# In-degrees counted by VectorE from the edge keys, and one zero piece stored in product 2, in a four-layer graph network

## The reference

```python
agg = jax.ops.segment_sum(h[src], dst, num_segments=n)          # products 0, 1, 2
...
deg = jax.ops.segment_sum(jnp.ones_like(dst, dtype=x.dtype), dst, num_segments=N)
agg = msg_sum / jnp.clip(deg, 1.0, None)[:, None]               # third stage
...
neigh2 = jax.ops.segment_sum(msg2, dst, num_segments=N) / jnp.maximum(deg, 1.0)[:, None]   # last stage
```

## Time and profile before

| | |
|---|---|
| median of three runs | 4858.66 us (4850.25 to 4870.81) |
| profiled execution | 4872.96 us, span of its instructions 4871.1 us |
| PE matmuls busy | 3396.0 us (70%) |
| VectorE busy | 2163.5 us (44%) |
| ScalarE busy | 1955.0 us (40%) |
| GpSimd busy | 1785.8 us (37%) |
| mean granted TensorE clock | 0.842 of 2.4 GHz |

### The profile page before, as it was taken

How to read it: one execution, slowest core, us unless ns; L and a number is a source line. 1 busy time by engine, 2 the same in 40 slices (tenths; PEclk the granted TensorE clock), 3 DMA queues, 4 the chain that set the end, 5 groups by cost and what they waited for, 6 DMA issues and landing times.

```text
span 4871.1 us, 57973 instructions
## 1 busy us (share of the span) xinstructions
PE 3396.0 (70%) x22119; PEld 2919.8 (60%) x22119; DVE 2163.5 (44%) x4433; ACT 1955.0 (40%) x3073; POOL 1785.8 (37%) x1727
## 2 busy tenths in 40 slices
PE   4798888711113997995119999983577777777788
PEld 2676777610113996994019989973465565555666
DVE  8786777510003986884002233242233333333335
ACT  5687878610001444454006546552222222222221
POOL 3000000177772000887760000005665555555630
PEclk9999999855556998996559989996799888888999
DMA  4888888700003677442004424423355555555555
GB/s 152 224 231 238 230 224 232 218 14 4 7 7 77 219 240 251 133 130 37 4 7 150 135 67 149 130 60 108 93 198 187 197 188 182 181 195 196 187 193 180
DMA packets 299723, 712.84 MB, mean 146 GB/s; under 512 B 65270, under 2 KB 167445, under 8 KB 284214
## 3 DMA queue, kind: packets, MB, share of 16 engines
q1 hardware_dynamic: 167180, 436.77, 28.3%
q10 hardware_dynamic: 52298, 174.64, 10.2%
q0 software_dynamic: 79968, 97.68, 9.4%
HBM read 503.59 MB, written 254.50 MB: 156 GB/s over the span
## 4 chain that ended last, share of the span: by engine, by line
PE 47%; another core or an unknown queue 23%; ACT 9%; issue 7%; DVE 7%; DMA 5%; ACTq 1%; DVEq 0%; POOL 0%; SPq 0%; POOLq 0%
PE PS L740 21%; PE PS L1725 7%; DMA turned<-DEG 4%; PE PS L662 4%; PE PS L1711 3%; ACT CA L859 2%; ACT DEG L884 2%; PE PS L1701 2%; PE PS L625 2%; PE PS L1693 2%; PE PS L671 1%; DVE BB L1877 1%; PE PS L718 1%; ACT BB L1811 1%
## 5 line engine op out<-in xcount | busy, mean ns | idle before, releaser
L431 POOL DMA_INDIRECT PAN<-table,src_i x832 | 828.3, 996 | 1353.0 <-DMA table<-DEG 768.1
L972 POOL DMA_INDIRECT shares<-dst_f,spare x832 | 888.2, 1068 | 735.1 <-ACTq L777 427.2
L740 PE MATMUL PS<-CX,XH 125*128 125x376 f32 x2000 | 477.4, 318 | 260.0 <-issue 127.7
L740 PE MATMUL PS<-CX,XL 125*128 125x376 f32 x2000 | 472.7, 315 | 145.1 <-issue 145.1
L1819 ACT ACTIVATE BB<-PS 128x1024 f32<-128x1024 f32 x104 | 106.6, 1025 | 948.5 <-PE PS L1701 473.7
L740 PEld LDWEIGHTS PS<-CX,XH 125*128 125x128 f32 x2000 | 321.1, 197 | 276.8 <-issue 161.2
L740 PEld LDWEIGHTS PS<-CX,XL 125*128 125x128 f32 x2000 | 321.4, 197 | 145.0 <-issue 145.0
L537 ACT ACTIVATE CX<-PAN 125x3125 fp32r<-125x3125 uint8 x106 | 298.2, 2814 | 270.0 <-PE PS L740 233.2
L740 PE MATMUL PS<-CP,XH 125*128 125x376 f32 (+1 forms) x1330 | 313.3, 315 | 124.0 <-issue 79.4
L740 PE MATMUL PS<-CP,XL 125*128 125x376 f32 (+1 forms) x1330 | 309.8, 312 | 63.4 <-issue 63.4
L884 ACT ACTIVATE DEG<-PS 125x1250 uint8<-125x1250 bf16 x250 | 303.0, 1212 | 113.0 <-PE PS L671 61.8
(11 more groups left out here) (334 smaller groups left out, 7026.8 us busy)
## 6 DMA issues: line engine op xcount, KB each, us to landing
PAN<-counts SPq DMA_DIRECT2D x300, 390.6 KB
shares<-SSB ACTq DMA_DIRECT2D x70, 1600.0 KB
XP<-shares SPq DMA_DIRECT2D x50, 1600.0 KB
PAN<-shares SPq DMA_DIRECT2D x50, 1600.0 KB
BB<-start_penalty SPq DMA_DIRECT2D x104, 512.0 KB
shares<-blank ACTq DMA_DIRECT2D x15, 3200.0 KB, 13.9
turned<-DEG SPq DMA_DIRECT2D x50, 781.2 KB, 9.7
PAN<-turned SPq DMA_DIRECT2D x100, 390.6 KB
```

The costliest lines, as they stand in the source:

```text
L431: nc.gpsimd.indirect_dma_start(out=gbuf[g % 2][:, k, :], out_offset=None, in_=source, in_offset=bass.IndirectOffsetOnAxis(ap=src_i[:, t:t ...
L740: last = nc.tensor.matmul(wide_ps[b][h][:, 0:w], halves[part][0:TN, s * SUBJ + j, :], cast_part(v, j, h), start=(s == 0 and j == 0 and par ...
L972: nc.gpsimd.indirect_dma_start(out=shares_flat, out_offset=bass.IndirectOffsetOnAxis(ap=share_at[:, t:t + 1], axis=0), in_=share[:, t:t + ...
```

## The change

VectorE counts the edges of each node from the keys of `dve_window_keys`: for each block and each of the five places in a window, one comparison with a sum (`window_degrees`), 50 in all. The evictions of `take_turn` no longer sum. The degrees lie by windows now (125 partitions, ten blocks, five places), so the store has runs of five elements, and ACT reads the row back by tiles of 125 in `act_in_mean` for use at the end. The build stores six pieces of zeros, three parts in a slice of either width; product 2 stores five slices, one with each of its blocks 0 to 4.

```diff
-ZBUILT = 7
-ZEROS_AT = {"dense1": (1,) * 10, "taken1": 5, "dense2": (0,) * 10}
+ZBUILT = 6
+ZERO_STEPS = tuple(NHI * (i + 1) // (ZBUILT - 2) for i in range(ZBUILT - 3))
+ZEROS_AT = {"dense1": (1,) * 10, "taken1": 5, "dense2": (1,) * 5 + (0,) * 5}
...
-        in_sums = DEG[0:TN, 5728:5728 + TURNS * NBLK * TPB].rearrange("p (c j) -> p c j", c=TURNS)
+        degree_win = DEG[:, 5728:5728 + NBLK * WIN].rearrange("p (q c) -> p q c", c=WIN)
+        degree_junk = DEG[:, 5792:5920]
...
                 if n == 1 and c == 0:
-                    store_degrees(act, 0, rin, rin_ready, rin_out)
+                    act.wait_ge(rin_ready, 1)
+                    act.dma_start(degree_rows[0:1, :].rearrange("o (q p c) -> p (o q) c", p=NWIN, c=WIN),
+                                  rin[0:NWIN, :].rearrange("p (q c) -> p q c", c=WIN)).then_inc(rin_out, 16)
...
                 nc.scalar.activation(to.rearrange("p (b k n) -> p b k n", b=2, n=TN),
-                                     turn_ps[turn_item(k, r) % 2][0:TN, :, :, 0:TN], ACT.Copy,
-                                     accum_out=in_sums[:, m, at:at + 1]).then_inc(turn_taken, 1)
+                                     turn_ps[turn_item(k, r) % 2][0:TN, :, :, 0:TN], ACT.Copy
+                                     ).then_inc(turn_taken, 1)
...
-                    if j in ((12, 24, 36) if k % 2 else (10, 20, 30, 40)):
+                    if j in ((12, 24, 36) if k % 2 else ZERO_STEPS):
                         blank_part()
...
+        def window_degrees(dve, first, count, local, c):
+
+            for x in range(count):
+                placed_after(dve, nc.vector.scalar_tensor_tensor(
+                    out=degree_junk, in0=local[:, x, :], scalar=iota[:, c:c + 1], in1=bc(ones[:, 0:1], 128),
+                    op0=ALU.is_equal, op1=ALU.mult, accum_out=degree_win[:, first + x, c:c + 1]))
...
             elif part == 6:
                 placed_after(dve, nc.vector.tensor_tensor(out=src, in0=src, in1=src_a, op=ALU.add))
+                window_degrees(dve, first, count, local, 0)
...
         def dve_in_degrees(dve):
 
-            dve.wait_ge(turn_taken, TURNS * NBLK * TPB)
-            nc.vector.tensor_reduce(out=rin[0:TN, :], in_=in_sums.rearrange("p c j -> p j c"), axis=AX.X, op=ALU.add)
-            dve.drain()
-            nc.vector.tensor_scalar(rin[0:TN, :], rin[0:TN, :], 1.0, None, ALU.max)
-            dve.drain()
-            nc.vector.reciprocal(rin[0:TN, :], rin[0:TN, :]).then_inc(rin_ready, 1)
+            placed_after(dve, nc.vector.tensor_scalar(rin[0:NWIN, :], degree_win[0:NWIN, :, :].rearrange("p q c -> p (q c)"),
+                                                      1.0, None, ALU.max))
+            nc.vector.reciprocal(rin[0:NWIN, :], rin[0:NWIN, :]).then_inc(rin_ready, 1)
...
         def act_in_mean(act):
 
             spread_degrees(act, 0, A[:, 0:N], rin_out, rin_spread)
+            act.dma_start(rin[0:TN, :], degree_rows[0:1, :].rearrange("o (j p) -> p (o j)", p=TN),
+                          allow_slow_non_contiguous=True).then_inc(rin_out, 16)
...
             keep_nodes(LAST)
+            act.wait_ge(rin_out, 32)
```

More of the change, by code:

```diff
@@ L1121, in dve_window_keys @@
                 placed_after(dve, nc.vector.tensor_copy(hi, whole_i))
+                window_degrees(dve, first, count, local, 1)
             elif part == 9:
@@ L1124, in dve_window_keys @@
                                                                  op0=ALU.mult, op1=ALU.add))
+                window_degrees(dve, first, count, local, 2)
             elif part == 10:
@@ L1127, in dve_window_keys @@
                                                                  op0=ALU.is_ge, op1=ALU.add))
+                window_degrees(dve, first, count, local, 3)
             elif part == 11:
+                window_degrees(dve, first, count, local, 4)
                 nc.vector.scalar_tensor_tensor(out=lo, in0=hi, scalar=-float(TN), in1=src, op0=ALU.mult, op1=ALU.add)
```

## The result

The kernel after takes **4939.85 us** (median of 4 runs, 4938.84 to 4955.68) where the kernel before, on the same chip, takes 4860.49 us (4850.25 to 4870.81). The ratio is 1.0171, 95% interval 1.0141 to 1.0201: slower by about 80 us, clear of the noise though under 2%. Forecast were 4948 us and +89.

The account below looks back on a forecast made before the run. TensorE was taken to bound wide build slices and products, ScalarE the narrow slices, scatter crawl the holes. +116 - 12 - 9 + 6 - 12 = +89 us on 4858.66 gave 4948 us, range 4876 to 4995.

Parts of the forecast that it names:

- The late scatter: Product 2: the scatter's second half starts 155 us later, so 97 columns move behind the product; +116 us.
- The price of 1.292 us a column: Hole after product 2: each column scattered there costs its full time, 272.6 / 211; 97 columns give +125 us of crawl.
- Rival A: After product 2: the crawl ends when product 3 streams, so the late scatter costs 0 to 10 us; 4832 us, 13%.
- The build: Build: ten zero parts removed shorten ScalarE's `turned` wait by 1.2 us a wide slice; -12 us, bounds 0 and -49.
- Rival B: Build: the `turned` waits vanish and all 22 us of ScalarE's reads count; +34 us in all, 4893 us, 12%.
- Accumulator reads: Build evictions: dropping each read saves ScalarE 0.09 us, counted only in the ten narrow slices; -9 us.
- Comparisons: Build: 50 VectorE compares of 0.4 us, +2 before the first pair and +4 in slice 2; +6 us.
- The store of the degrees: Start of product 1: 1250 descriptors instead of 6250 shorten the next DMA issue from 16.78 to 3.4 us; -12 us.
- Stores in product 2 and the reload: Product 2's five added stores lie beside TensorE, product 4's degree reload has only casts after it; 0 each, reload bound +17.

Follow-up runs that it names:

- zeros_in_p1: Against the kernel after: the five zero stores of product 2 are issued in product 1 instead; 4838.17 us, ratio 0.9895 to the kernel before.
- zeros_only: The kernel before with only the new zeros (six pieces in the build, five stores in product 2), old degree counting and store; 4927.43 us, ratio 1.0098.
- degrees_only: The kernel after with the zeros of the kernel before, so only the VectorE degree counting and new store change; 4858.64 us, ratio 0.9965.

## Why the prediction came out as it did

**The late scatter: right, in place and size.** The second half was to start at the end of block 5's casts, 155 us later relative to product 2; it came 153.4 us later (2018.92 - 1930.02 + 64.5). The price of 1.292 us a column, less what TensorE does in it, gave +116; measured 119.7, and `zeros_in_p1` gives about 113 back. Rival A falls: between the steps TensorE crawled on to 2622.90, 23.8 us past the last column.

**The build: right in sign, three times too small.** The step that failed reads "The `turned` store has 2 us more before a third transfer joins. I take 1.2 us a slice". Measured are 5 us a wide slice, of which 3.6 are the wait that I had named (49.4 to 13.1 us in all). I had the right wait and its bound (-49), then sized it by how much later one store is issued, when what mattered was that four stores beside the slice's own transfers were one too many. The two parts run apart put it on the piece of zeros: 45.1 us of this wait with four stores, 11.4 with three. The other sign of it was in the earlier trace rows: TensorE busy 41.05 of 45.20 us at a DMA share of 0.94, so 4 us a slice to be had. (The prediction's "PE and ACT are between 88% and 93% busy" does not hold for ScalarE in the wide slices, 33.40 of 45.20 us or 74%.) With the store gone TensorE's own time fell as well, from 41.05 to 39.56 us, at a granted clock of 0.96 before and 1.00 after: that is the rest of the 5 us. Rival B, which had this, is the better account of the build: it gave -82 with the store, measured -64, though of its 22 us for the reads only 5.6 came.

**Accumulator reads: right in price, in seven of the ten narrow slices.** 0.8 us a narrow slice (37.90 to 37.14) against 0.9 forecast. It is the reads: these slices take 37.9 us in all four kernels that keep them, `zeros_only` among them, and 37.1 to 37.4 in the ten without, `degrees_only` among them. That makes -5.6 where ten slices were to give -9.

**Comparisons: the price right, a slice overlooked.** 0.40 us each as forecast. The first matmul of the first pair comes 1.7 us later (61.65 to 63.31), against +2. Then slice 2 has to be judged with the zeros held equal: it ended at 190.0 to 192.0 in the three kernels with the build of before and at 196.8 in `degrees_only`, at 187.8 in `zeros_only` and at 192.9 to 196.6 with both parts, some 2 us of which is the late start. So the 4 us are there, within a spread of 2 us. And slice 4, which I had taken to have room, went from 38.9 us to 41.5 or, in two kernels, 42.3 wherever the comparisons are made. In sum +2, +4 and +2.5 against -5.6 make about +3 where I had -3 (-9 + 6). `zeros_only` against the kernels with both parts gives +4 to +6; `degrees_only` by itself starts its scatter within the spread of those three (940.71 against 940.4 to 946.0).

**The store of the degrees: right.** The issue fell to 5.66 us (a fifth, 3.4, was forecast; it is a third), and the start of product 1 gained 11 to 12 us (12 forecast).

**Stores in product 2 and the reload: right at nothing.** From product 1 to block 1 of product 2 the difference moves by 0.2 us, to block 6 (2092.15 and 2027.61), behind all five stores, by no more, and from product 3 to the first gather by -3.8.

**The sum was nearer than its terms.** The build came out 37 us lower than forecast and the way from product 3 to the first gather 4 us, and against that stand 4 us more in the hole, the 15 us of the last stage which no step of mine holds, and an execution of before 12.5 us over its median. The forecast of +89 was met by +79, partly by luck.

**What couples the scatter to TensorE** was left open and stays open in one part. Shown is that columns with more room between them free TensorE, by degrees, and that GpSimd's own work between them is not what frees it. Not shown are whether the distance, the pause or the number of columns on their way counts, and what the two engines share. That it is TensorE's supply of instructions is argued only from the idle time for which the trace names no awaited engine. The Trainium skill (Runtime: NRT & Kernel Launch, Instruction fetch mechanics) says that each engine fetches its instructions ahead through a DMA queue of its own and that this is mostly hidden. If that supply is what fails, the trace disagrees where columns follow at 1.28 us, with 18 matmuls in 50 us, and agrees where they follow at 2.2 us, with 420 in 80. But late fetches alone do not fit the rows. The profile has this line on the busier of the two queues for instructions:

```profile
q8 instruction: 181, 2.97, 0.2%
```

That is 16.4 KB a packet. By an estimate one holds some 250 instructions (3.74 MB in both queues for 57,818 instructions, 65 B each). A packet that comes late would make one long pause and then a burst; in the hole the instructions come singly, 1.4 us or so apart, for 22 us beyond the last column too.

## What to carry to other kernels

One engine can slow another here with no semaphore, no busy queue and almost no bytes between them: where an engine idles on "issue" and another issues small transfers back to back, try these transfers further apart before anything else is tuned, and then look for the pace at which the scatter itself does not come last. Here one short write of 0.17 us behind each column was worth 16%, where the change under study moved 2%. And when a store is taken out of a stage that is close to two limits, compare the stage's length with the busy time of its fullest engine. In the one case here that difference was 4.2 us and the store gave 5.0, where its bytes said 6.4 (1.6 MB at 254 GB/s) and the shift of its issue 1.2.

## What the runs showed of the hardware

- Indirect scatters of 128 elements each, 1.28 to 1.40 us apart with little other traffic, hold TensorE to one instruction, a matmul or a weight load, in about 1.4 us: 18 matmuls in 50 us. In the gap between products 3 and 4 it does 205 matmuls in 80 us beside scatters 1.42 us apart, 420 beside scatters 2.2 us apart or waiting for each other's landing, and 415 with none.
- The crawl outlasts the last column's start by 22 to 24 us (22.4 before, 23.8 after) with DMA share 0.00.
- Beside a streaming product (130 GB/s and more) a column takes 1.6 us in place of 1.28 by itself, and with three writes between the columns 2.52 us in place of 2.11, in the mean over both halves.
- A DMA issue behind a store of 6250 elements of 4 B took 16.78 to 16.96 us; behind a store of the same bytes in runs of five elements, 5.66 to 5.84 us.
